# Reordering the query-only end of a linear-attention kernel and moving four transposes to another PSUM bank

## What is computed

```python
qkv = x @ Wqkv + bqkv                      # x: (8, 2048, 512), 16 heads of 32
q_prime = exp(q @ omega - 0.5 * sum(q*q))  # omega: (32, 128); k_prime likewise
k_sum   = sum(k_prime, over the sequence)
k_v     = einsum('bhnm,bhnd->bhmd', k_prime, v)
out     = (q_prime @ k_v) / (q_prime @ k_sum + 1e-6)
x = layernorm(x + out @ Wout + bout)
x = layernorm(x + x @ weight.T + pooled(x) @ disha)
```

## Time and profile before

| what | value |
|---|---|
| median of 3 runs | 2447.77 us |
| profiled execution, its own time | 2453.35 us |
| its span, first to last instruction | 2451.6 us |
| PE, DVE, ACT, POOL busy, share of the span | 96%, 81%, 52%, 12% |
| full slot | 73.4 to 75.8 us |
| slot 32; 33; 34; 35; 36 with the last store | 66.5; 50.5; 48.4; 45.5; 23.4 us |

### The profile page before, as it was taken

How to read it: one execution, slowest core, us unless ns; L and a number is a source line. 1 busy time by engine, 2 the same in 40 slices (tenths; PEclk the granted TensorE clock), 3 DMA queues, 4 the chain that set the end, 5 groups by cost and what they waited for, 6 DMA issues and landing times.

```text
span 2451.6 us, 55233 instructions
## 1 busy us (share of the span) xinstructions
PE 2364.0 (96%) x21224; PEld 1326.1 (54%) x21224; DVE 1984.2 (81%) x4007; ACT 1265.7 (52%) x2281; POOL 291.1 (12%) x390
## 2 busy tenths in 40 slices
...
DMA packets 160277, 213.11 MB, mean 87 GB/s; under 512 B 19376, under 2 KB 119824, under 8 KB 156048
## 3 DMA queue, kind: packets, MB, share of 16 engines
...
...
## 4 chain that ended last, share of the span: by engine, by line
PE 61%; DVE 22%; issue 8%; ACT 5%; SPq 1%; POOL 1%; DMA 1%; DVEq 0%; POOLq 0%; ACTq 0%
PE bank_a L450 18%; PE bank_y L450 13%; PE bank_x L450 13%; DVE q_feat_lo L825 3%; DVE k_feat_lo L818 3%; PE bank_qf L569 3%; PE bank_x L610 3%; PE bank_kf L515 2%; DVE xt_lo L938 2%; DVE stats L770 2%; PE kv_ps L541 2%; DVE yt_lo L883 2%; DVE v_both L812 1%; PE bank_nm L593 1%; DVE nm_f L863 1%
## 5 line engine op out<-in xcount | busy, mean ns | idle before, releaser
L678 ACT ACTIVATE k_feat<-bank_kf 128x512 f32<-128x512 f32 x512 | 305.8, 597 | 255.1 <-PE bank_kf L515 223.8
L688 ACT ACTIVATE q_feat<-bank_qf 128x512 f32<-128x512 f32 x512 | 304.9, 595 | 177.1 <-PE bank_qf L569 176.6
L818 DVE TENSOR_TENSOR k_feat_lo<-k_feat 128x512 bf16<-128x512 f32 x512 | 369.6, 722 | 19.5 <-ACT k_feat L678 19.1
L825 DVE TENSOR_TENSOR q_feat_lo<-q_feat 128x512 bf16<-128x512 f32 x512 | 352.5, 695 | 33.2 <-ACT q_feat L688 28.7
L969 POOL TENSOR_TENSOR rstd<-mean_var,minus_half 128x1 f32<-128x1 f32 x128 | 82.8, 647 | 1687.3 <-DVE mean_var L901 1687.3
L958 POOL TENSOR_TENSOR rows<-rows,bias_out 128x512 f32<-128x512 f32 x128 | 165.9, 1308 | 456.3 <-DMA rows<-x 456.3
L515 PE MATMUL bank_kf<-omega_s,stack_k 98*128 98x128 f16 x1920 | 185.9, 219 | 3.4 <-ACT k_feat L678 3.0
L569 PE MATMUL bank_qf<-stack_q,omega_s 98*128 98x256 f16 x960 | 184.4, 273 | 4.1 <-ACT q_feat L688 3.2
L541 PE MATMUL kv_ps<-v_both,k_feat 128*128 128x65 f16 (+1 forms) x2048 | 181.4, 190 | 4.8 <-DVE k_feat_lo L818 4.8
L515 PEld LDWEIGHTS bank_kf<-omega_s,stack_k 98*128 98x128 f16 x1920 | 137.9, 97 | 85.7 <-issue 23.5
L547 PE MATMUL kv_ps<-v_both,k_feat_lo 128*128 128x33 f16 x2048 | 182.7, 179 | 0.0
...
## 6 DMA issues: line engine op xcount, KB each, us to landing
rows<-x SPq DMA_DIRECT2D x128, 256.0 KB, 2.9
out<-rows SPq DMA_DIRECT2D x128, 256.0 KB, 2.0
...
```

What stands on the lines that cost most here:

```text
L678: nc.scalar.activation(k_feat[:, i % 2, :], bank_kf[:, :], ACT.Exp, scale=1.0 / WS).then_inc(S["k_exp"], 1)
L688: nc.scalar.activation(q_feat[:, 2 * pair:2 * pair + 2, :], bank_qf[:, :].rearrange("p (e n) -> p e n", e=2), ACT.Exp, scale=1.0 / WS).the ...
L818: v.tensor_tensor(k_feat_lo[:, u, :], k_feat[:, u, :], k_feat_hi[:, u, :], ALU.subtract).then_inc(S["kfl"], 1)
L825: v.tensor_tensor(q_feat_lo[:, at, :], q_feat[:, at, :], q_feat_hi[:, at, :], ALU.subtract).then_inc(S["qfl"], 1)
```

## The change

Four things. (1) Slots 32 to 34 get new texts, and slots 35 and 36 become one, with a text of its own (`ORDER_END`); slot 36 is empty. (2) In full chunks AT3 and YT2 write bank_nm, the numerators' bank, in place of bank_x; for chunk 27, whose primed pieces stand in slot 32, AT2 and YT3 do too. Waits are added so that numerators and transposes don't meet there. (3) FF3 of chunk 27 goes to kv_ps1, after KFIN1. (4) In full slots NM5 stands ahead of KV5 and KF6 instead of behind them. The matmuls themselves are the same, 21224 of them.

```diff
-KF3 WO1. ... VP3. VP3 KV4 NM4 XL1 FF0. KF5 YT1 XL2 FF0 XL3 KV5 KF6
-NM5
+KF3 WO1. ... VP3. VP3 KV4 NM4 XL1 FF0. KF5 YT1 XL2 FF0 XL3 NM5 KV5 KF6
...
 ORDER_Q = """
-QP0. AT2' NM6' NM7' QP0 QF0 WO2'. QF1 WO2' AT3' Z1' QF2 QP1. YT2' QF3 QP1 QF4 WO3'. QF5 WO3' QF6 FF2'. ...
+QP0. AT2' NM6' NM7' QP0 WO2'. QF0 WO2' AT3' QF1 QP1. Z1' QF2 QP1 YT2' QF3 WO3'. QF4 WO3' QF5 FF2'. ...
...
+ORDER_END = """
+AT2' NM6' NM7' QF0 WO2'. QF1 WO2' AT3' QF2 WO3'. Z1' QF3 WO3' YT2' QF4 FF2'. QF5 FF2' QF6 YT3' QF7 FF3'. ...
...
             if kind == "FF" and (CPB * b + c >= CPB * B or CPB * b + c == CPB * B - 1 and i > 0):
-                return kv_ps[1] if alone(b, c) and i % 2 else bank_a
+                return kv_ps[1] if i % 2 and (alone(b, c) or i == 3) else bank_a
             if alone(b, c) and kind in ("AT", "YT"):
                 return kv_ps[0]
+            if (kind, i) in (("AT", 3), ("YT", 2)) or CPB * b + c == CPB * B - 1 and (kind, i) in (("AT", 2), ("YT", 3)):
+                return bank_nm
             return bank_y if kind in ("WO", "FF") else bank_x
...
             if b == B:
-                return 4 if c else 2
+                return (2, 4, 4, 6, 7)[c]
...
                         wait(pe, "nm_sum", 8 * j + i)
+                        if i == 0 and j > 0:
+                            wait(pe, "yt_lo_done", TPC * j - 1)
+                        if j == LAST_Q - 1 and i == 6:
+                            wait(pe, "at_lo_done", TPC * j + 3)
```

More of the change, by code:

```diff
@@ L67 @@
 QP2 FF3'. NM1 FF3' VP1. AT0 NM2 Z3' KF0 VP1 QF8 NM3 WO0. KF1 QF9 WO0 KV0 KF2 VP2. AT1 KV1 QF10 VP2 QF11
-KF3 WO1. QF12 YT0 KV2 QF13 WO1 QF14 QP3. KF4 QF15 XS QP3 KV3 XL0 VP3. VP3 KV4 NM4 XL1 FF0. KF5 YT1 XL2 FF0 XL3 KV5 KF6
-NM5
+KF3 WO1. QF12 YT0 KV2 QF13 WO1 QF14 QP3. KF4 QF15 XS QP3 KV3 XL0 VP3. VP3 KV4 NM4 XL1 FF0. KF5 YT1 XL2 FF0 XL3 NM5 KV5 KF6
 """
@@ L88 @@
 ORDER_LAST = """
[L89 to L92, removed]
+KF7' QN' KV6' Z0' FF1'. KF8' KV7' FF1' AT2' KF9' KV8' QP0. Z1' KF10' NM6' KV9' QP0 QF0 KF11' NM7' KV10' WO2'. QF1 KF12' KV11' WO2' QF2
+AT3' KF13' KV12' QP1. KF14' QF3 KV13' QP1 YT2' KF15' QF4 KV14' WO3'. QF5 WO3' KV15' KFIN0' KFIN1' QF6 FF2'. YT3' QF7 FF2' QP2.
+QP2 NM0 NM1 FF3'. AT0 NM2 NM3 FF3' Z2' QF8 WO0. QF9 WO0 AT1 QF10 Z3' QP3. QF11 QP3 YT0 QF12 WO1. QF13 WO1 QF14 FF0.
+QF15 FF0 YT1 QN NM4 NM5 Z0 FF1. FF1
 """
 ORDER_Q = """
-QP0. AT2' NM6' NM7' QP0 QF0 WO2'. QF1 WO2' AT3' Z1' QF2 QP1. YT2' QF3 QP1 QF4 WO3'. QF5 WO3' QF6 FF2'. QF7 YT3'
-FF2' QP2. NM0 NM1 QP2 FF3'. AT0 NM2 NM3 FF3' QF8 WO0. Z2' QF9 WO0 AT1 QF10 QP3. YT0 QF11 QP3 Z3' QF12 WO1. QF13
-WO1 QF14 FF0. QF15 YT1 FF0 QN NM4 NM5 Z0 FF1. FF1
+QP0. AT2' NM6' NM7' QP0 WO2'. QF0 WO2' AT3' QF1 QP1. Z1' QF2 QP1 YT2' QF3 WO3'. QF4 WO3' QF5 FF2'. QF6 FF2' YT3' QF7 QP2.
+QP2 NM0 NM1 FF3'. Z2' NM2 NM3 FF3' AT0 QF8 QP3. QF9 QP3 AT1 QF10 WO0. Z3' QF11 WO0 QF12 WO1. QF13 YT0 WO1 QF14 FF0. QF15
+FF0 YT1 QN NM4 NM5 Z0 FF1. FF1
+"""
+ORDER_END = """
+AT2' NM6' NM7' QF0 WO2'. QF1 WO2' AT3' QF2 WO3'. Z1' QF3 WO3' YT2' QF4 FF2'. QF5 FF2' QF6 YT3' QF7 FF3'. FF3' NM0
+NM1 NM2 NM3 AT0 Z2' QF8 WO0. QF9 AT1 WO0 QF10 QF11 WO1. QF12 YT0 QF13 WO1 QF14 FF0. QF15 Z3' FF0 YT1 NM4 NM5 FF1. AT2 FF1 NM6
+NM7 Z0 WO2. WO2 AT3 Z1 WO3. YT2 WO3 FF2. FF2 YT3 Z2 FF3. FF3 Z3
 """
```

10 lines of the change are left out of this document (7 added, 3 removed).

## The result

The changed kernel takes 2414.4 us (median of 4 runs, 2413.8 to 2416.0) against 2449.2 for the kernel before beside it: ratio 0.9867, 95% interval 0.9854 to 0.9879. Measured again beside the experiments it was 2414.5, ratio 0.9859 (0.9839 to 0.9878). So 33 to 35 us came off; the prediction had 22, and its range ended at 2417.

What follows compares the result with a forecast made beforehand. PE was taken to bound full slots (72.8 of 73.7 us busy), leaving mainly end waits to gain. 3 + 6.7 + 5.8 + 8.4 - 1.7 = 22.2 us off gave 2426 us; 8-in-10 range 2417 to 2439.

Steps and rivals of the forecast that it cites:

- The step that failed: Full slots: NM5 ahead of KV5 covers a 0.1 us wait, which AT2 behind the norms' read-out takes back; gain 0.
- Full slots, the bank: Full slots: with AT3 out of bank_x QP0 no longer waits for its low part; 3.5 us at most, 3 taken.
- Slots 32 to 36: Last slots: reordering removes waits on PE; 6.7 us in slot 32, 5.8 in 33 and 34, 8.4 in 35 and 36.
- Half clock: Last slots: one stretch of PE at 1.2 instead of 2.4 GHz stays, costing 1.7 us.
- rival 2: Slots 32 to 35: many short waits drop the clock five times instead of once, 6.8 us more, 2433; chance 0.07.
- 1 (DVE the bound): Last slots: DVE becomes the bound, slot 32 gives 2 us, 13 us gained in all, 2435; chance 0.13.
- 3 (KF6's low part delays KV6): Full slots: KF6's low part behind NM5's operations makes KV6 wait, slower, up to 42 us, 2468; chance 0.04.
- 4: Banks do nothing and QF0 waits as now for chunk 31's DMAs: 17 us gained, 2431; inside the forecast's 0.70.
- 5: Whole kernel: waits move one for one and the time stays within 0.3% of before; chance 0.06.

Runs made afterwards that it cites:

- run 3: Kernel before with NM5 ahead of KV5 and KF6 in full slots for PE, ACT and GpSimd only, DVE's order as before: 2450.1 us, ratio 1.0006.
- run 4: Kernel before with NM5 ahead of KF6's low part in DVE's full-slot order alone, other engines as before: 2434.8 us, ratio 0.9949.
- run 1: Kernel before with only NM5 moved ahead of KV5 and KF6 in full slots, all engines following: 2438.7 us, ratio 0.9965.
- run 2: Kernel before with only AT3 and YT2 of full chunks in bank_nm and the waits for it, texts unchanged: 2444.9 us, ratio 0.9986.
- Run 5: Kernel before with the change's orders of slots 32 to 36 and its last chunk's banks, full slots as before: 2427.2 us, ratio 0.9916.
- run 9: Changed kernel with one more small GpSimd operation between FF0's power op and shift in every full slot: 2439.8 us, ratio 0.9964.

## Why the prediction was wrong

**The step that failed** is "NM5 ahead of KV5 covers a wait of KV5 of 0.1 us, but AT2 behind it waits for the norms' read-out, which hangs on DVE and not on PE, and takes it back: 0". The link that it names is right: AT2 waited 9.4 us in 27 slots for the read-out of the norms from bank_x, which DVE does. For PE's order alone the 0 is right too, and in the way described: in run 3 KV5's waits fell by 2.5 us, AT2's rose by 2.3, and the time stayed. What failed is that I took the time of that read-out as given. The move reorders DVE as well, and the chain that ends in the read-out starts two engines further back, with a GpSimd operation on 128 numbers that DVE's old order had stretched from 0.55 to 0.94 us. By runs 3 and 4 PE's order is worth nothing and DVE's everything. The step's price by run 1 is 8.6 us and not 0; by run 4, 12.4.

**Full slots, the bank: right.** 3 predicted, 2.5 measured at QP0 (run 2), by the mechanism named: PE from AT3 to QP0 0.1 us less. The other rows forecast for it came in only by halves: full slots of 73.1 and not 73.4, yt_lo at 15.3 where "near 17" was said.

**Slots 32 to 36: right, nearly term by term.** 6.1 for 6.7, 5.8 for 5.8, 7.1 for 8.4 less half clock. Of the waits, as idle time in the timeline: NM0 2.3 for 2.3, KV13 1.4 for 1.9, KV12 0.4 for 0.55, QF4 in the query-only slots 0.1 and 0.4 for 0.65, last AT2 0.8 for 0.85. Run 5, the ends alone, gives 20.6 us for the 19.2 of the sum.

**Half clock: about right in total.** I kept one stretch at 1.7 us. This trace of the changed kernel has two ahead of its tail, behind NM0's wait and in slot 35:

```profile
2232.40:2235.80 3.40, 3.40 (x31) 1.78 (x28) 2.28 (x9) 0.00 (x0) 2.98 (x4) 0.50 0.01 2
2372.30:2375.70 3.40, 3.07 (x10) 0.98 (x9) 2.41 (x6) 1.75 (x3) 0.41 (x1) 0.51 0.22 80
```

The second trace of the same kernel (the repeat beside run 9) has the first and not the second, and there slots 35 and 36 took 60.6 us for 61.8: that stretch cost 1.2 us, and whether it comes differs from run to run. Kernel 5, with the same text of slots 32 to 36, has neither; its slot 32 took 59.6 us for 60.3, so the first stretch cost at most 0.7 (0.3 of it is a wait of KV6 that kernel 5 doesn't have). Both are under the 1.7 us of the prediction; that part of a stretch falls on waits would explain it, but no run here shows it. Ahead of the second one no wait in slot 35 was over 1.0 us, where in the kernel before the stretch of that slot stood behind one of 2.45. That is rival 2 on a small scale: one stretch more than forecast in one of two traces, worth about 1 us and not 6.8.

**Rivals.** 1 (DVE the bound) fell: slots 33 and 34 gave all of their 5.8, slot 32 6.1 and not 2. 3 (KF6's low part delays KV6) is answered the other way round: its being later is what gained, and KV6 waited only 0.7 us over the 27 slots together. 4 and 5 fell with runs 2 and 5.

**The range** failed with the term. With the full slots at 3 + 8.6 the sum is 30.8 us, and the time 2417 from the median shown: the edge of the range. The 2 to 3 us from there to 2414.4 no run places. I had given the move's upside no bound, only its downside, though a row of the waits of the kernel before was there to bound it, and names the right releaser:

```profile
PE bank_x L610 <- DVE half_norm L792: 6.1, 28, 1.1
```

It counts only PE's idle time; the piece-by-piece sum at AT2 is 9.4, for part of the wait lies under matmuls that still run out.
